# The ragged item of an edge loop: one overlapping item becomes one short item

## The reference, cut to what matters

```python
# N = 625 nodes, D = 512 = 16 segments of 32, 20000 edges sorted by dst, 64 paths
def gnn(x_nodes, x_edges, path_coeffs, src, dst, path_indices):
    x1 = x_nodes[src].reshape(-1, 16, 32)          # one gathered row per edge
    x2 = x_edges.reshape(-1, 16, 32)               # one loaded row per edge
    i1, i2, i3 = path_indices.T
    contrib = path_coeffs[None, :, None] * x1[:, i1, :] * x2[:, i2, :]
    edge_out = zeros(E, 16, 32).at[:, i3, :].add(contrib)
    return zeros(N, 512).at[dst].add(edge_out.reshape(-1, 512))

x = x + gnn(layernorm(x), edge_attr, path_coeffs, src, dst, path_indices)
x = x + ffn(layernorm(x))   # 2 shared experts, 64 routed experts, top 6, plus its own input
```

## Time and profile before

| | |
|---|---|
| median of 3 runs | 1124.46 us (1121.32 to 1127.37) |
| profiled execution | 1130.64 us |
| its span, first to last instruction | 1129.3 us |
| mean granted TensorE clock | 0.943 |
| DVE busy | 568.0 us (50%), 1307 instructions |
| PE busy | 906.7 us (80%), 7256 instructions |
| POOL busy | 386.3 us (34%) |
| multiplications of the messages (L565) | x640, 391.7 us |
| DMA | 322.77 MB, mean 286 GB/s |

### The profile page before, as it was taken

One profiled execution on the slowest core, in us unless ns is written; L12 is line 12 of the kernel. 1 busy time (PEld: TensorE's weight loads), 2 busy tenths in 40 slices (PEclk: granted clock), 3 DMA queues, 4 the chain that ended last, 5 costly groups with the idle time before them and its releaser, 6 DMA issues.

```text
span 1129.3 us, 20457 instructions
## 1 busy us (share of the span) xinstructions
PE 906.7 (80%) x7256; PEld 495.9 (44%) x7257; DVE 568.0 (50%) x1307; ACT 228.2 (20%) x582; POOL 386.3 (34%) x421
## 2 busy tenths in 40 slices
PE   0057776676677777788999999999999969999986
PEld 0033343343333343555464454544546436454473
DVE  5099999999999999444111111121111111111126
ACT  0122222332232131131111211122111111111100
POOL 2643354336334520027743223233232322322210
PEclk9997999999999989758799999999999989999998
DMA  7944576567557653826699999999999999999756
GB/s 250 338 134 152 174 241 216 198 215 251 196 197 243 207 180 149 310 93 233 235 314 386 393 398 398 397 387 399 392 395 394 370 401 396 394 392 395 287 135 196
DMA packets 76573, 322.77 MB, mean 286 GB/s; under 512 B 18875, under 2 KB 19028, under 8 KB 54418
## 3 DMA queue, kind: packets, MB, share of 16 engines
q1 hardware_dynamic: 52176, 259.90, 61.5%
q0 software_dynamic: 22432, 57.44, 15.7%
q10 hardware_dynamic: 1826, 3.54, 1.0%
HBM read 310.15 MB, written 13.63 MB: 287 GB/s over the span
## 4 chain that ended last, share of the span: by engine, by line
PE 64%; DVE 13%; issue 8%; DVEq 7%; DMA 4%; ACT 2%; POOL 1%; SPq 1%; ACTq 0%; POOLq 0%
PE ps L1091 22%; PE ps L1137 11%; DVE big L565 10%; PE ps L582 8%; PE ps L1163 5%; PE ps L1040 4%; DVEq L556 3%; DVEq L563 3%; DMA big<-y_d 2%; PE ps L1181 2%; PE ps L1084 2%; PE ps L616 2%; PE ps L632 2%; PE ps L894 1%; PE ps L1111 1%
## 5 line engine op out<-in xcount | busy, mean ns | idle before, releaser
L565 DVE TENSOR_TENSOR big<-big 128x512 f32 x640 | 391.7, 689 | 30.5 <-DMA big<-xn_d,idx 26.5
L1091 PE MATMUL ps<-big 128*64 128x512 f32 x1024 | 248.0, 629 | 18.6 <-issue 17.5
L582 PE MATMUL ps<-big,mixed 128*32 128x256 f32 x2560 | 170.7, 412 | 104.2 <-DVE big L565 104.2
L324 POOL DMA_INDIRECT big<-xn_d,idx x160 | 169.6, 1060 | 223.1 <-DVE big L565 161.6
L1101 DVE TENSOR_TENSOR mixed<-big,ps 128x256 f32<-128x256 f32 x64 | 27.0, 421 | 287.7 <-ACT big L1098 287.7
L582 PEld LDWEIGHTS ps<-big,mixed 128*32 128x32 f32 x2560 | 79.9, 117 | 189.8 <-DVE big L565 78.2
L1091 PEld LDWEIGHTS ps<-big 128*64 128x64 f32 x1024 | 71.2, 143 | 151.1 <-issue 145.8
L990 POOL DMA_INDIRECT big<-h_d,Lg x52 | 50.8, 977 | 251.2 <-issue 249.6
L1137 PE MATMUL ps<-big,mixed 128*64 128x256 f32 x1024 | 127.0, 391 | 1.6 <-issue 1.6
L1057 POOL DMA_INDIRECT y_d<-big,sia x74 | 75.3, 1018 | 107.5 <-DVE big L1150 97.5
L1137 PEld LDWEIGHTS ps<-big,mixed 128*64 128x64 f32 x1024 | 68.8, 138 | 37.7 <-issue 5.7
(11 more groups left out here) (193 smaller groups left out, 736.8 us busy)
## 6 DMA issues: line engine op xcount, KB each, us to landing
big<-in_L_ffn_Wg SPq DMA_DIRECT2D x64, 1024.0 KB, 17.6
big<-in_L_ffn_Wu SPq DMA_DIRECT2D x64, 1024.0 KB, 22.0
big<-in_L_ffn_Wd SPq DMA_DIRECT2D x64, 1024.0 KB, 17.3
big<-in_edge_attr SPq DMA_DIRECT2D x40, 1024.0 KB, 5.9
big<-y_d SPq DMA_DIRECT2D x10, 672.0 KB
big<-xn_d,idx POOLq DMA_INDIRECT x160
big<-in_L_ffn_sWg SPq DMA_DIRECT2D x2, 1024.0 KB, 6.0
big<-in_L_ffn_sWu SPq DMA_DIRECT2D x2, 1024.0 KB, 8.1
```

The costliest lines, as they stand in the source:

```text
L324: pool.indirect_dma_start(xs[s][:, c, :], None, xn_d[:, :], bass.IndirectOffsetOnAxis(ap=table[:, c0 + c:c0 + c + 1], axis=0)).then_inc(x_ ...
L565: ins = dve.tensor_tensor(pr[k % 2][:, :, EXT * p:EXT * (p + 1)], xs[s][:, :, ds(o1, EXT)], es[s][:, :, ds(o2, EXT)], ALU.mult)
L582: ins = pe.matmul(bank(BA)[WIN * h:WIN * (h + 1), h0:h0 + HP * EXT], onehot[s][:, CW * h + r, :], pr[k % 2][:, CW * h + r, :], start=r == ...
L1091: ins = pe.matmul(bank(k2)[TA * h:TA * (h + 1), :].rearrange("p (w f) -> p w f", w=2), xgT[k2][:, k, 0:TA], gu[:, :, k, W * h:W * (h + 1)] ...
```

## The change

The item that is not full moves from the end to the front, and it holds only its own edges. Item 0 has `SHORT` = 20000 - 9 x 2048 = 1568 edges: three full quarters (`FQ` = 3) and a fourth of `REST` = 32 edges, which lie one to a lane in lanes 0 to 31 of one chunk. That makes `EC0` = 13 chunks. Items 1 to 9 are full and start at 1568, 3616 and so on. The other 96 lanes of chunk 12 get `dst` = -1, source 0 (they gather row 0) and edge values 0. `one_hots`, `products`, `contract` and `gather_sources` take the number of chunks. `src` and `dst` are now each loaded by three transfers, the third of them with a stride (4 bytes at a time). ACT's queue waits for a new memset of `src_r`, SP's queue for POOL's setup ahead of item 0's edges. The loop that does not run here has its body twice now, once for item 0 and once for the others.

```diff
-    LAST = NE_EDGES - GE
-    DUP = NG * GE - NE_EDGES
+    SHORT = NE_EDGES - (NG - 1) * GE
+    FQ, REST = divmod(SHORT, QE)
+    EC0 = CW * FQ + 1
...
+            if short and h == FQ:
+                sync.dma_start(es[s][0:REST, CW * FQ, :], edge_attr[FQ * QE:SHORT, :]).then_inc(e_in[s], 16)
...
-    def gather_sources(s, table, c0, until=None):
-        for c in range(EC):
+    def gather_sources(s, table, c0, until=None, chunks=EC):
+        for c in range(chunks):
...
+    g_src = G(pool.memset(src_r[0:QW, :], 0))
...
+    G(pool.memset(es[0][:, CW * FQ, :], 0.0))
...
-    V(dve.memset(dst_r[:, :], -1))
+    def by_lane(r):
+        return r[FQ:QW, :].rearrange("g (p r) -> g p r", r=CW)[:, 0:REST, 0]
+
+    V(dve.memset(dst_r[0:QW, :], -1))
     after(act, V)
+    act.wait_ge(G.sem, g_src)
+
+    def load_ends(name, r, ends):
+        return load(act, name,
+                    (r[QW:NR, :], ends[SHORT:NE_EDGES].rearrange("(g e) -> g e", e=QE)),
+                    (r[0:FQ, :], ends[0:FQ * QE].rearrange("(g e) -> g e", e=QE)),
+                    (by_lane(r), ends[FQ * QE:SHORT].rearrange("(g e) -> g e", g=1)), strided=True)
+
+    s_src, n_src = load_ends("ld_src", src_r, src)
+    s_dst, n_dst = load_ends("ld_dst", dst_r, dst)
...
     sync.wait_ge(s_x, n_x)
-    load_edges(0, 0)
+    sync.wait_ge(G.sem, g_const)
+    load_edges(0, 0, short=True)
...
-    load_edges(1, GE)
+    load_edges(1, SHORT)
...
-    gather_sources(0, idx, 0)
+    gather_sources(0, idx, 0, chunks=EC0)
     gather_sources(1, idx, EC)
...
-                ins = dve.tensor_tensor(pr[k % 2][:, :, EXT * p:EXT * (p + 1)],
-                                        xs[s][:, :, ds(o1, EXT)], es[s][:, :, ds(o2, EXT)], ALU.mult)
+                ins = dve.tensor_tensor(pr[k % 2][:, 0:chunks, EXT * p:EXT * (p + 1)],
+                                        xs[s][:, 0:chunks, ds(o1, EXT)], es[s][:, 0:chunks, ds(o2, EXT)], ALU.mult)
...
         for r in range(CW):
             for h in range(QW):
+                if CW * h + r >= chunks:
+                    continue
...
-            first = LAST if t + 1 == NG - 1 else (t + 1) * GE
-            load_edges(1 - s, first, SUB * t)
+            load_edges(1 - s, SHORT + t * GE, SUB * t)
```

More of the change, by code:

```diff
@@ L84, in gnn_moe @@
     assert N == NB * BP and TCR <= P
-    assert DUP < QE and NG % 2 == 0 and NR <= P
+    assert FQ == QW - 1 and 0 < REST <= P and NG % 2 == 0 and NR <= P
     def sb(name, shape, dt=F32):
@@ L308, in gnn_moe, with load_edges @@
     x_in = [sem(f"x_in{k}") for k in (0, 1)]
-    def load_edges(s, first, until=None):
+    def load_edges(s, first, until=None, short=False):
         for h in range(QW):
@@ L372, in gnn_moe @@
                          base=QW - 1, pattern=[[QW, NG]], channel_multiplier=-1))
-    G(pool.memset(gtab[:, NG - 1:NG], LAST))
     G(pool.memset(fill[:, :, 0:2], 1 << 20))
     g_const = G.n
-    V(dve.memset(dst_r[:, :], -1))
+    def by_lane(r):
+        return r[FQ:QW, :].rearrange("g (p r) -> g p r", r=CW)[:, 0:REST, 0]
+    V(dve.memset(dst_r[0:QW, :], -1))
     after(act, V)
[L380 to L388, removed]
+    act.wait_ge(G.sem, g_src)
[6 more added lines that the diff above has]
+    s_dst, n_dst = load_ends("ld_dst", dst_r, dst)
     s_pi, n_pi = load(act, "ld_paths", (praw[:, :], path_indices.rearrange("(a n) c -> a (n c)", a=1)))
@@ L532, in at, with one_hots @@
         return isinstance(t, int) and t in of
-    def one_hots(t, s, bias):
+    def one_hots(t, s, bias, chunks=EC):
         if not at(t, 0, 1):
             act.wait_ge(part_used, SUB * t - SUB)
-        for c in range(EC):
+        for c in range(chunks):
             ins = act.activation(onehot[s][:, c, :], iotaw[:, 0:WIN], ACT.Abs, bias=bias(c))
@@ L541, in one_hots @@
         act.wait_ge(oh_ab, t + 1)
-        act.activation(onehot[s], onehot[s], ACT.Relu, scale=-1.0, bias=ones[:, 0:1]).then_inc(oh_ok, 1)
+        act.activation(onehot[s][:, 0:chunks, :], onehot[s][:, 0:chunks, :], ACT.Relu, scale=-1.0,
+                       bias=ones[:, 0:1]).then_inc(oh_ok, 1)
     def place_rows(t, bias):
@@ L550, in place_rows, with products @@
         act.activation(place, place, ACT.Relu, scale=-1.0, bias=ones[:, 0:1]).then_inc(place_ok, 1)
-    def products(t, s, edges, sources):
+    def products(t, s, edges, sources, chunks=EC):
         for k in range(SUB):
@@ L570, in products, with contract @@
                     dve.memset(opening[:, PER * k + p // PER:PER * k + p // PER + 1], 0.0)
-    def contract(t, s, k):
+    def contract(t, s, k, chunks=EC):
         h0 = HP * EXT * (k % 2)
@@ L581, in contract @@
             for h in range(QW):
+                if CW * h + r >= chunks:
+                    continue
                 ins = pe.matmul(bank(BA)[WIN * h:WIN * (h + 1), h0:h0 + HP * EXT], onehot[s][:, CW * h + r, :],
-                                pr[k % 2][:, CW * h + r, :], start=r == 0, stop=r == CW - 1)
+                                pr[k % 2][:, CW * h + r, :], start=r == 0,
+                                stop=r == min(CW, chunks - CW * h) - 1)
         ins.then_inc(part_used, 1)
@@ L641, in gnn_moe @@
     after(act, G, g_const)
-    one_hots(0, 0, lambda c: wdst[:, c:c + 1])
+    one_hots(0, 0, lambda c: wdst[:, c:c + 1], EC0)
     dve.wait_ge(s_xn, n_xn)
@@ L649, in gnn_moe @@
         if 0 < t < NG - 1:
-            first = LAST if t + 1 == NG - 1 else (t + 1) * GE
-            load_edges(1 - s, first, SUB * t)
+            load_edges(1 - s, SHORT + t * GE, SUB * t)
             gather_sources(1 - s, idx, EC * (t + 1), SUB * t)
-        products(t, s, 16 * QW * (t // 2 + 1), 16 * EC * (t // 2) + 16 * EC)
+        chunks = EC if t else EC0
+        products(t, s, 16 * QW * (t // 2 + 1), 16 * EC * (t // 2) + 16 * (EC if s else EC0), chunks)
         for qq in range(PARTS):
-            contract(t, s, 2 * qq)
-            contract(t, s, 2 * qq + 1)
+            contract(t, s, 2 * qq, chunks)
+            contract(t, s, 2 * qq + 1, chunks)
             evict(t, qq)
@@ L700, in gnn_moe, with more_item @@
     dve.nop().then_inc(added_ok, 1)
+    def more_item(j, g, first, chunks):
+        x = j * NG + g
+        t = x + NG
+        c0 = g * EC
+        load_edges(1, first, short=chunks < EC)
+        pool.wait_ge(part_ok, SUB * t)
+        pool_ready()
+        pool.tensor_copy(idxx[:, :], idx[:, ds(c0, EC)]).then_inc(idxx_ok, 1)
+        pool.wait_ge(idxx_ok, x + 1)
+        pool_ready()
+        gather_sources(1, idxx, 0, chunks=chunks)
+        dve.wait_ge(put_ok, NB * t)
+        dve.wait_ge(added_ok, NB * x + 1)
+        for b in range(NB):
+            add_block(b).then_inc(added_ok, 1)
+        dve.tensor_scalar(wdx[:, :], wdst[:, ds(c0, EC)], woff[:, ds(j + 1, 1)], None, ALU.add)
+        dve.tensor_scalar(nrx[:, :], nrow[:, ds(g, 1)], woff[:, ds(j + 1, 1)], None, ALU.subtract
+                          ).then_inc(more_ok, 1)
+        products(t, 1, 16 * QW * (NG // 2 + x + 1),
+                 16 * EC * (NG // 2) + 16 * EC0 + j * (16 * EC0 + 16 * EC * (NG - 1)) + 16 * EC * g, chunks)
+        act.wait_ge(more_ok, x + 1)
+        one_hots(t, 1, lambda c: wdx[:, c:c + 1], chunks)
+        place_rows(t, nrx[:, :])
+        for qq in range(PARTS):
+            contract(t, 1, 2 * qq, chunks)
+            contract(t, 1, 2 * qq + 1, chunks)
+            evict(t, qq)
+            turn(t, qq)
+            evict_turned(t, qq)
+            select(t, qq)
+        evict_sums(t)
+        pe.wait_ge(added_ok, NB * x + NB + 1)
+        put(t, range(NB), start=True, stop=True)
@@ L701, in gnn_moe @@
     with nc.If(nmax > 0):
         with nc.Fori(0, nmax) as j:
[L703 to L734, removed]
@@ L736, in gnn_moe @@
+            sync.wait_ge(part_ok, SUB * (j * NG + NG))
+            more_item(j, 0, 0, EC0)
+            with nc.Fori(1, NG) as g:
+                first = sync.value_load(gtab[0:1, ds(g, 1)], min_val=0, max_val=NE_EDGES - GE)
+                sync.wait_ge(part_ok, SUB * (j * NG + g + NG))
+                more_item(j, g, first, EC)
     nput = nmax * (NG * NB) + NG * NB
```

9 lines of the change are left out of this document (5 added, 4 removed).

## The result

The changed kernel takes **1114.1 us** (median of 7 runs, 1111.44 to 1120.12), the kernel before beside it 1125.65 (7 runs, 1121.32 to 1129.54). The ratio is 0.991, 95% interval 0.9889 to 0.9932: 0.9% faster, about 10 us. The forecast was 1116.5, in a range of 1110 to 1123.

The account below looks back on a forecast made before the run. DVE was taken to bound item 0's products, with a chain of waits ahead of them. Terms +0.4 - 2.1 - 6.4 + 1.0 - 0.9 = -8.0 us off the median 1124.46 gave 1116.5 us, range 1110 to 1123.

Parts of the forecast that it names:

- The start: Ahead of item 0: one more transfer queued before `dst` delays its landing, +0.4 us (0 to +1.1).
- the products: Item 0's 64 multiplications on DVE cover 416 instead of 512 elements a lane, saving 6.4 us.
- The two terms on PE: Item 0: +1.0 us for DVE waiting in the first pair, -0.9 us for half the later wait going.
- The gathers: Item 0 needs 13 gathers, not 16; DMA backlog is the bound: -2.1 us, down to -3.75 were POOL the bound.
- PE behind it: Item 0's contractions on PE keep their time with 13 chunks, so DVE may wait: +1.0 and -0.9 us.
- +1.0 for the first pair: Item 0's first pair of parts: DVE waits for PE starting at the lower clock, +1.0 us (0 to +3.7).
- -1.85 behind item 0: DVE's wait for PE before item 1 may go if the clock stays up; half counted, -0.9 us (0 to -1.85).
- A: Rival: PE takes over in item 0 at the lower clock, 1125.3 us; with one more low pair 1120; chance 0.15 for either.
- B: Rival: padding is dear, by same-row gather, sequencer or strided loads; a gather of 8.4 us gives 1123.8 us; chance 0.08.
- C: Rival: later items meet PE's clock at another phase; eight more low pairs give 1131.3 us; chance 0.04.
- The expert stage: Behind the message stage: it moves as a whole, its span of 669 us changing by no more than 2 us.
- The signs of being wrong: Contraction shrinks, DVE waits for PE in more than one pair of item 0, or expert stage's span changes over 2 us.

Follow-up runs that it names:

- e1: Changed kernel with item 0 gathering 16 chunks again, three of them ordinary rows nobody multiplies; ratio 0.9934 to the kernel before.
- the repeats: Kernel before and changed kernel, each run twice more without edit on other chips; ratios 1.0025 and 0.9908, the second run of each without a ratio.
- e4: Changed kernel with item 1's edges issued only when all 13 gathers of item 0 have landed; ratio 0.9967 to the kernel before.
- r_after: Changed kernel again, no edit, on another chip beside the kernel before; ratio 0.9908 to it.
- r_after2: Changed kernel once more, no edit, one run at 1172.93 us; the kernel before there took 1179.04 us.
- e5: Kernel before with the short item of 13 chunks last (item 9) and item 0 full; ratio 0.9934 to the kernel before.
- e7: Changed kernel with item 1's gathers sent three at a time as item 0's parts are done; ratio 0.9845 to the kernel before, 1160.06 us against 1179.04.
- e8: Changed kernel with item 1's gathers paced, padding lanes on rows 0 to 511 and item 1's edge transfers split; ratio 0.9853 to the kernel before.

## Why the prediction was right

The forecast was -8.0 us, and the ratio says -10.1 (-7.7 to -12.5 by its interval). The start and the products, which carry the forecast, came as the prediction had them, each somewhat larger: together 9.6 us by the first traces. The two terms on PE nearly cancel (+1.0 - 0.9), so the total says little about them; that part was luck.

- **The start.** +0.4 for the landing of `dst`: measured 0. The transfer came later and landed as before. Here the added transfer of 128 bytes was not on the path, although the queue was.
- **The gathers.** -2.1 by the backlog of the DMA engines, not -3.75 by POOL: -2.7 in the first pair, 2.03 in e1, 1.2 and 2.4 between the repeats. The choice of the bound was right, and looking at the queue by stretches decided it. Two small parts were not in the sum: the same-row lanes cost an estimated 0.4 us (the prediction had 0 to 0.5), and in e4 a gather took 4.0 us to land with the engines busy for 66 to 75% only.
- **The products.** -6.4: measured 39.26 - 32.4 = 6.9. The multiplications run 0.506 us apart instead of 0.607 (0.101 each, 6.5 in all), as the slope of two rows said. Of the other 0.4 some 0.3 is the tiny memsets: a part with three of them took 0.08 us longer than one without before, and 0.03 now (8.10 and 8.04 for two). The sequencer stayed hidden.
- **PE behind it.** The contraction did not shrink with the chunks: 26 records in 1.93 us. The Trainium skill (TensorE: Matmul & The Clock Gate, "Part 3: Packing small matmuls — row/col tiling") lets different column tiles run concurrently, and the trace agrees. The +1.0 for the first pair (the prediction's own working, 9.0 against 8.3, gives 0.7) was not paid, and the clock had risen by the second contraction (3.39, then 1.93 us); the -1.85 behind item 0 came in full, and the wait of 1.74 in item 1, which the forecast left alone, went too, against a new one of 0.2 in item 9. These three make 3.5 of the 4.9 us by which the message stage of the first pair of traces beats the sum (the start and the products make the rest). They are the part that the repeats do not hold up: elsewhere the waits in item 0 were 9.5 to 11.7 us, in both kernels, and the message stages differed by 7.2 and 7.9 us, which is start and products (9.3 and 8.1) less 2.1 and 0.2 us. Whether shorter parts keep the clock up is therefore not settled.
- **Rivals.** A (PE takes over in item 0) did not come in the first trace. It was given waits of 3.7, 3.4 and 3.4 us; r_after shows 3.65, 3.15 and 3.61, but the likeness is chance. A had them ahead of the third pair, the fourth and item 1, from PE at the lower clock; r_after has them ahead of the third part, the fourth and the fifth, the second of them behind a contraction whose records end at 63.92. The kernel before lost 11.7 us in item 0 there too, so the products' gain was not eaten. What the argument lacked is that a rival's price has to be taken in both kernels. B: the same row is dear, at 0.56 us a gather and not 7.7. C did not come.
- **The expert stage** moved as a whole, within its scatter of 7 us from trace to trace (664.7 to 671.5).
- **The signs of being wrong.** One of the three was met: the prediction called itself wrong if the expert stage's span changed by more than 2 us, and it changed by 4.3 in the first pair of traces. The sign was too tight, since one kernel's span there moves by more (666.1 to 670.3 for the kernel before, in three traces). In r_after and r_after2 a second one was met, waits for PE in more than one pair of item 0, and again in the kernel before as well.

## What to carry to other kernels

Where one engine is the bound and processes padded or repeated items, its share is simply elements times the slope between two shapes of the same instruction, and it comes off in full when the engines behind it have time to spare; check that their work shrinks too, or how much they have. A ragged item that is put first also has smaller transfers for the fill of the pipeline: the first product came 1.2 to 2.7 us sooner here, which the totals of e5 and of the changed kernel do not tell apart. And a start that waits for transfers is decided by who else uses the DMA engines at that time: read the queues by stretches of a few us before taking the issuing engine for the bound.

## What was not expected of the hardware

- PE's matmuls, or the eviction behind a contraction whose records are complete, can come up to 10 us late with nothing that the profile shows to wait for, in some surroundings and not in others, in the kernel before as in the changed one. Ten of the twelve traces after the first comparison lost 9.5 to 13.7 us so in item 0; with 16 gathers held back for 5.5 us the loss was 0 (e7) or 4.5 us (e8).
- An indirect gather whose 128 lanes all read one row of 2 KB took 0.56 us longer than one of different rows, which took 0.68 us in the full queue (by one trace of each kind).
